# Moving ternary rounding, feature-attention normalisation and masked memory keys from VectorE to GpSimd

## The reference

```python
x = x + attention(layernorm(x))                  # 16 heads of 128, softmax over tokens
x = x + linear_attention(layernorm(x), ctx)      # relu features, divided by their sums
x = x + gated_ffn(layernorm(x))                  # weights quantised to nf4 and back
e = einsum('bci,bcj->bij', xn, xn)               # xn = layernorm(x)
x = x + einsum('bcj,bij->bci', xn, softmax(e))   # attention over features
x = x + gate * memory_attention(rmsnorm(layernorm(x)), ctx, mask)   # 16 heads of 16, 64 keys
x = x + ternary_ffn(layernorm(x))
```

```python
h = square(relu(h)); xmax = maximum(max(h, axis=-1), eps)
h = round(h / xmax * 255) / 255 * xmax
out = h @ w2.T
```

## Time and profile before

| | |
|---|---|
| median of 3 runs | 932.9 us (932.67 to 932.92) |
| the profiled execution, by its own count | 934.24 us |
| its span in the trace | 932.4 us |
| TensorE busy | 858.7 us, 92% |
| VectorE busy | 729.2 us, 78% |
| ScalarE busy | 520.5 us, 56% |
| GpSimd busy | 369.0 us, 40% |
| mean granted TensorE clock | 0.98 of full speed |

### The profile page before, as it was taken

How to read it: one execution, slowest core, us unless ns; L and a number is a source line. 1 busy time by engine, 2 the same in 40 slices (tenths; PEclk the granted TensorE clock), 3 DMA queues, 4 the chain that set the end, 5 groups by cost and what they waited for, 6 DMA issues and landing times. The chain is left out here.

```text
span 932.4 us, 18697 instructions
## 1 busy us (share of the span) xinstructions
PE 858.7 (92%) x6868; PEld 637.5 (68%) x6868; DVE 729.2 (78%) x1777; ACT 520.5 (56%) x1245; POOL 369.0 (40%) x356
## 2 busy tenths in 40 slices
PE   4798998999999999999999986999988889999786
PEld 3455766777777777777777765787856568777554
DVE  5738867878888788887887745898798879887895
ACT  1435576656665566656665643554364863535556
POOL 3104455545555555545554553044133031522410
PEclk9889999999999999999999997999999999999999
DMA  9022331011101111011100000000000010000001
GB/s 285 32 65 68 55 93 35 2 35 34 34 7 27 34 34 34 0 34 34 34 5 6 1 1 1 1 2 1 1 2 1 1 46 2 1 1 1 1 1 46
DMA packets 34722, 25.56 MB, mean 27 GB/s; under 512 B 9492, under 2 KB 31596, under 8 KB 34668
## 3 DMA queue, kind: packets, MB, share of 16 engines
q1 hardware_dynamic: 34380, 24.56, 10.1%
q10 hardware_dynamic: 288, 0.26, 0.1%
HBM read 22.65 MB, written 2.17 MB: 27 GB/s over the span
## 5 line engine op out<-in xcount | busy, mean ns | idle before, releaser
L476 POOL CAST exp_hi<-exp_scores 128x1024 f16<-128x1024 f32 x64 | 67.0, 1047 | 217.9 <-ACT exp_scores L580 217.9
L74 PE MATMUL banks<-value_out_hi,xn_t_hi 128*128 128x256 f16 x512 | 140.8, 275 | 2.3 <-DVE X L874 2.3
L478 POOL TENSOR_TENSOR exp_lo<-exp_scores,exp_hi 128x1024 f16<-128x1024 f32 x64 | 140.7, 2198 | 5.1
L580 ACT ACTIVATE exp_scores<-banks,exp_bias,unscale 128x256 f32<-128x256 f32 x256 | 141.0, 560 | 2.1
L75 PE MATMUL banks<-value_out_lo,xn_t_hi 128*128 128x256 f16 x512 | 140.6, 275 | 0.0
L76 PE MATMUL banks<-value_out_hi,xn_t_lo 128*128 128x256 f16 x512 | 140.6, 275 | 0.0
L1064 PE MATMUL banks<-qk 128*128 128x256 f32 x512 | 122.7, 383 | 9.9 <-ACT exp_scores L580 9.9
L1064 PEld LDWEIGHTS banks<-qk 128*128 128x128 f32 x512 | 97.2, 191 | 31.4 <-issue 10.5
L874 DVE SCALAR_TENSOR_TENSOR X<-banks,colsum,X 128x256 f32<-128x256 f32 x256 | 106.2, 477 | 11.0 <-DVE colsum L865 9.6
L562 ACT ACTIVATE qk<-banks 128x512 f32<-128x512 f32 x128 | 75.8, 601 | 59.1 <-PE banks L76 59.1
L853 DVE TENSOR_REDUCE neg_rowmax<-banks 128x4 f32<-128x1024 f32 x64 | 78.1, 1221 | 31.4 <-PE banks L1064 31.4
(11 more groups left out here) (238 smaller groups left out, 1965.9 us busy)
## 6 DMA issues: line engine op xcount, KB each, us to landing
head_weights<-in_wqkv_d SPq DMA_DIRECT2D x32, 128.0 KB, 3.7
weight_absmax_rows<-across_partitions SPq DMA_DIRECT2D x15, 256.0 KB, 4.1
X<-in_x_d SPq DMA_DIRECT2D x4, 512.0 KB, 7.5
head_weights<-in_wqkvt_d SPq DMA_DIRECT2D x16, 128.0 KB, 3.4
head_weights<-in_w_o_d SPq DMA_DIRECT2D x16, 128.0 KB, 3.5
out<-X SPq DMA_DIRECT2D x8, 256.0 KB, 2.1
res_then_ternary_then_kv<-in_c_fc_d SPq DMA_DIRECT2D x1, 1024.0 KB, 6.5
res_then_ternary_then_kv<-in_c_proj_d SPq DMA_DIRECT2D x1, 1024.0 KB, 8.2
```

What stands on the lines that cost most here:

```text
L74: nc.tensor.matmul(out, lhs[0], rhs[0], start=first, stop=False)
L476: nc.gpsimd.tensor_copy(probh[:, s1_.par], prob[:, s1_.par]).then_inc(exph_ready, 1)
L478: nc.gpsimd.tensor_tensor(probl[:, s1_.par], prob[:, s1_.par], probh[:, s1_.par], ALU.subtract).then_inc(expl_ready, 1)
L580: last = nc.scalar.activation(prob[:, s1_.par, t, :], sc_ps[t // ST][:, t % ST, :], ACT.Exp, bias=nbias[:, t:t + 1], scale=unscale[:, s1_. ...
```

## The change

Three steps are moved from VectorE to GpSimd. `fat_p` becomes one product of 128x512 with the two reciprocals spread over it. `mem_kbd` keeps its two products and gains explicit waits, one for the head mask and one for the sample's `fat_add`, which VectorE's order had implied. `n` is the same instruction on the other engine. The list of work names the new engine and new estimated lengths, so `turns_by_engine` gives new orders for all four engines.

```diff
--- before.py
+++ after.py
@@ -1235,10 +1235,10 @@
                 work += [f"ffn_{name}{m} {length} {after}"]
     work += [f"ffn_out PE 3.03 ffn_lo{FFT - 1}", "ffn_add DVE .67"]
     work += norm_work("fat", "ffn_add", ["xt ACT .49", "e PE 1.74 fat_xn"])
-    work += ["fat_max DVE .61", "fat_exp ACT .9", "fat_rsum DVE .08", "fat_p DVE .52", "fat_pt PE .45 fat_p fat_xt",
+    work += ["fat_max DVE .61", "fat_exp ACT .9", "fat_rsum DVE .08", "fat_p POOL 1.2", "fat_pt PE .45 fat_p fat_xt",
              "fat_pte ACT .49", "fat_out PE 1.83", "fat_add DVE .6"]
     work += norm_work("mem", "fat_add", ["xt ACT .74"])
-    work += ["mem_q PE 1.8", "mem_kbd DVE .67 fat_add", "mem_g PE 1.74 mem_xt", "mem_qt ACT .49 mem_q", "mem_ge ACT .49 mem_g"]
+    work += ["mem_q PE 1.8", "mem_kbd POOL 1.3 fat_add", "mem_g PE 1.74 mem_xt", "mem_qt ACT .49 mem_q", "mem_ge ACT .49 mem_g"]
     for t in range(ST):
         work += [f"mem{t}_{w}" for w in ("s PE 1.19" + (" mem_qt mem_kbd mem_ge" if t == 0 else ""),
                                          "max DVE 1.13", "sub DVE 1.14", "exp ACT .96", "sum DVE 1.13", "rd DVE .17",
@@ -1248,7 +1248,7 @@
     for t in range(ST):
         work += [f"ter{t}_{w}" for w in ("h PE 1.74" + (" ter0_nte ter0_add" if t else ""), "max DVE 1.13", "m0 DVE .12",
                                          f"relu ACT 1.0 ter{t}_max", f"c0 DVE .24 ter{t}_m0", "c1 DVE .08",
-                                         f"sq ACT 1.04 ter{t}_relu ter{t}_c1", "n DVE .6", "nt PE .45", "nte ACT .91",
+                                         f"sq ACT 1.04 ter{t}_relu ter{t}_c1", "n POOL 1.1", "nt PE .45", "nte ACT .91",
                                          "out PE .9", "add DVE .4")]
     turns = turns_by_engine(work)
 
@@ -1292,6 +1292,24 @@
                 pool.wait_ge(mem_rden[t], n[s])
                 nc.gpsimd.tensor_tensor(by_head(s), by_head(s), den[s][:, t, :].unsqueeze(2).broadcast_to([P, XH, M]),
                                         ALU.mult).then_inc(mem_pn[t], 1)
+            elif name == "fat_p":
+                pool.wait_ge(fat_rsum, n[s])
+                nc.gpsimd.tensor_tensor(att[s][:, :, :], att[s][:, :, :],
+                                        small[s][:, 2:4].unsqueeze(2).broadcast_to([P, KT, D]),
+                                        ALU.mult).then_inc(fat_p, 1)
+            elif name == "mem_kbd":
+
+                pool.wait_ge(mask4_ready, 1)
+                pool.wait_ge(fat["added"], n[s])
+                for k in range(KT):
+                    last = nc.gpsimd.tensor_tensor(
+                        kbd[s][:, k], g.k1t[:, k, M * s:M * (s + 1)].unsqueeze(1).broadcast_to([P, HK // 2, M]),
+                        g.mask4[:, :].unsqueeze(2).broadcast_to([P, HK // 2, M]), ALU.mult)
+                last.then_inc(mem_kbd, 1)
+            elif part == "n":
+                t = tile_of(layer)
+                pool.wait_ge(ter_sq[t], n[s])
+                nc.gpsimd.tensor_scalar(num[s], hid[s], ROUND, -ROUND, ALU.add, ALU.add).then_inc(ter_n[t], 1)
             elif name == "lin_bias":
 
                 pool.wait_ge(lin["xn"], n[s])
@@ -1499,22 +1517,9 @@
             elif name == "fat_rsum":
                 dve.wait_ge(fat_exp, n[s])
                 nc.vector.reciprocal(small[s][:, 2:4], small[s][:, 2:4]).then_inc(fat_rsum, 1)
-            elif name == "fat_p":
-                dve.wait_ge(fat_rsum, n[s])
-                for t in range(KT):
-                    last = nc.vector.tensor_scalar(att[s][:, t, :], att[s][:, t, :], small[s][:, 2 + t:3 + t], None,
-                                                   ALU.mult)
-                last.then_inc(fat_p, 1)
             elif name == "fat_add":
                 add_bank(s, fat_out, PB, "fat")
 
-            elif name == "mem_kbd":
-
-                for k in range(KT):
-                    last = nc.vector.tensor_tensor(
-                        kbd[s][:, k], g.k1t[:, k, M * s:M * (s + 1)].unsqueeze(1).broadcast_to([P, HK // 2, M]),
-                        g.mask4[:, :].unsqueeze(2).broadcast_to([P, HK // 2, M]), ALU.mult)
-                last.then_inc(mem_kbd, 1)
             elif name == "mem_go":
 
                 dve.wait_ge(mem_out, n[s])
@@ -1564,9 +1569,6 @@
                 dve.wait_ge(ter_step[s], s // STREAMS * 3 * ST + 3 * t + 2)
                 nc.vector.tensor_scalar(small[s][:, 7:8], small[s][:, 6:7], float(np.sqrt(255.0)), None,
                                         ALU.mult).then_inc(ter_scale[t], 1)
-            elif part == "n":
-                dve.wait_ge(ter_sq[t], n[s])
-                nc.vector.tensor_scalar(num[s], hid[s], ROUND, -ROUND, ALU.add, ALU.add).then_inc(ter_n[t], 1)
             elif part == "add":
                 dve.wait_ge(ter_step[s], s // STREAMS * 3 * ST + 3 * t + 3)
                 dve.wait_ge(ter_out[t], n[s])
```

## The result

The changed kernel takes **954.6 us** (median of 4 runs, 951.99 to 955.57) against 932.8 before (932.67 to 932.92): ratio **1.0234 [1.0216, 1.0252]**, 21.8 us slower. The prediction had 936.8 and a range to 940.5. The time moved the way that was forecast, but more than five times as far, and most of it for another reason than the one that the forecast priced.

A forecast was written before the change was run, and what follows sets the result against it. TensorE was taken to set the pace, except VectorE in memory attention and the four engines' hand-over in the ternary layer. Terms 1.4 + 0 + 2.5 = +3.9 us on 932.9 gave 936.8 us, range 932.0 to 940.5.

The forecast's parts named there:

- slow rival: Rounding costs 2.2 us or more on GpSimd and every collision is paid in full: 938.9 to 940.3 us; chance 0.12.
- collisions: VectorE's normalising pass waits for the GpSimd mask product of the same sample: 0 to 1.1 us for each sample.
- D's last transposes: Sample 7, end of last ternary layer: rounding's extra 0.4 us hides behind TensorE's order; at 2.2 us, 0.35 later.
- Place one: Between features and memory, each wave: mask product ahead of sample 3's scaling, pass collisions; +0.7 a wave, +1.4 in all.
- Place two: Between the waves: second wave's first samples fill TensorE, and a small delay is gained back; 0, bounds -0.5 and +1.4.
- Place three: Last wave's ternary layer: new orders delay additions, copies and second-half products; +2.5 us, bounds +1.0 and +3.5.
- No change: Rival: an earlier start of the ternary layer makes good the orders' losses there; 932.9 us, 931.0 to 934.8; chance 0.13.
- the sign that it asked for: No change's condition: VectorE's release before 680 us reaches the memory stretch, 2 to 3 us earlier.
- Faster: Rival: GpSimd starts roundings on time, reordering costs nothing, TensorE's 4.0 us of waits for roundings go: 928.9 us; chance 0.13.
- Slower still: The slow rival: rounding 2.2 us or more, collisions paid in full; 938.9 us, or 940.3 with place two; chance 0.12.
- the forecast's own walk: Step-by-step timing of the last wave's ternary layer, rounding taken as 1.1 us on GpSimd; it gave +2.5 us.

The follow-up runs named there:

- r_forms: The changed kernel with the rounding step in eight forms, by sample and half of the tokens; ran once, only instruction lengths read, no kernel time given.
- r_forms3: Third such kernel against the changed one: eight more forms of the instruction, f32 in, f16 out, 128x1024; ran once, only instruction lengths read.
- r_cast: The changed kernel with GpSimd's rounding replaced by a plain cast to f16 (1.04 us), all orders kept: 932.9 us, ratio 1.0009 against before.
- r_conv: The changed kernel with ScalarE's square written as 32-bit integers and GpSimd copying them to f16: 932.6 us, ratio 1.0009 against before.
- r_fma: The changed kernel with the rounding as one multiply-add on GpSimd, ScalarE's copy taking 1024 off: 933.3 us, ratio 1.0011 against before.
- r_two: The changed kernel with the rounding as two GpSimd copies, to 32-bit integers and back to f16 (2.08 us): 934.75 us, +2.8 against before.
- r_back: The changed kernel with the rounding back on VectorE, orders made anew; scalings and mask products stay on GpSimd: 933.0 us, ratio 1.0012 against before.
- r_none_moved: The kernel of r_none with scalings and mask products moved to GpSimd: 928.59 us, ratio 0.9949 against before.
- r_none_again: The same kernel as r_none, timed once more beside r_none_moved: 924.63 us, ratio 0.9915 against before.
- r_conv_last: As r_conv, with wave two's ternary layer in the order of before on TensorE, VectorE and ScalarE: 931.6 us, ratio 0.9999 against before.
- r_none: The kernel before without any rounding instruction: ScalarE writes 16-bit integers, TensorE transposes their bits, ScalarE's copy converts: 924.35 us, ratio 0.9910.

## Why the prediction was wrong

**The step that failed is one term: "Rounding, 128x1024 f32 to f16 with one input: the cast of that shape takes 1047 ns ... I take 1.1, nearest the cast (one input), and keep 1.05 to 2.2."** It was mis-sized by 2.5 us for each of 16 instructions. A cast and a two-operation arithmetic instruction share shape, types and the number of inputs, and the forecast took that to be enough. On GpSimd the operations decide (r_forms to r_forms3): the same shape costs 1.04 or 3.63. The bound of 2.2 was no bound either: it came from a row with a subtraction of two inputs, and an instruction with one input was taken to lie below it. No row of before had a tensor_scalar with arithmetic on that engine at this shape, so both ends were guesses. The slow rival said "2.2 us or more", but its time was worked out at 2.2, and "much more" had no price.
The Trainium skill (GPSIMD Engine Reference, 4.1 Engine selection) calls one-input work roughly line-rate, and its key points say that VectorE is about 2 times faster for elementwise work (1.37 us by that, an estimate). Neither agrees with 3.63 against 0.684 us, a factor of 5.3; the forms of 1.04 lie between.

**The direction was in the main luck.** The forecast's +3.9 was made of orders and collisions. With a rounding of 1.04 these gave +0.7 to +1.6 (r_cast, r_conv, r_fma), and over 20 of the 21.8 us came from a length that the forecast had hidden behind TensorE's order.

**What followed from a wrong size.** The text said that at 2.2 us D's last transposes start 0.35 later. That looked at one rounding, the last. r_two (2.08) lost 1.9 us in S against r_conv, and 1.5 of them lie before hA: four first-half roundings arrive close together, and the slow rival priced none of that. It also had the clock falling only as part of a bound of one microsecond, where the same matmuls took 9.1 us longer. In the change the last layer lost 11.0: hA starts 15.2 us after the last power, not 9.7 (+5.5), and from hA to the last addition it takes 26.3, not 20.8 (+5.5, in which hA at half clock is 1.7 longer and a wait for a rounding near the end is 3.07).

**Place one, +1.4 (0 to 2.5).** Right, in mechanism and nearly in size. The wait of 0.35 us before sample 3's transposes was seen (forecast 0 to 0.8), and so were the projection ahead of the output product and the collisions: where a pass met the mask products of its sample it took 1.0 to 1.3 us in place of 0.7, well under the upper bound. The waits are 1.6 (r_back against before) to 1.9 us (r_none_moved against r_none_again) for both waves. The 2.9 by which the second pair's P and R differ has 1.0 of longer matmuls in it, for which place one had no term.
The Trainium skill (SBUF — State Buffer, SBUF: two separate sides) calls the shared ports an exclusive lock for a whole instruction. The trace agrees, down to two columns: a step of 0.15 us took 1.73 and ended with the 1.90 of GpSimd. It does not bear out the full 1.1 that the prediction drew from it: with the first of the two mask products over, the pass went ahead, 0.3 to 0.6 us late. VectorE's row maxima, which read PSUM, kept their 1.22 us beside 14.4 us of GpSimd's roundings.

**Place two, 0 (-0.5 to +1.4).** Wrong: with a short rounding the new order gains 1.7 us there (Q, r_cast and r_conv_last). TensorE's idle time in Q and R together is 15.8 us in r_back and 14.3 to 14.4 in r_cast and r_conv. The prediction gave VectorE's 5.5 us of roundings no worth there, although in Q VectorE serves the first wave's ternary layer and the second wave's first layers at once. Whether the relief or the new order gains it, no run separates.

**Place three, +2.5 (1.0 to 3.5).** Right in sign, at the lower bound in size: +1.0 (r_conv against before), and r_conv_last takes it away again. r_cast's S alone (+2.6) had seemed to confirm 2.5; 1.6 of it was a dip. The three places together, read as TensorE's idle time, come to +1.0 (32.4 before, 33.4 to 33.6 in r_cast, r_conv and r_fma): +1.1 in P, -1.1 in Q and R, +0.9 in S.

**Rivals.** No change was what the moves gave with a short rounding (+0.7 to +1.6 in r_cast, r_conv and r_fma), and the sign that it asked for was there: counted from the first power, the last layer starts 328.1 us on in before, 327.0 in r_conv and 325.9 in r_cast. But that came through Q, where 1.7 us were gained, and through a dip in R that before has and these two have not, and not through the memory stretch. Faster saw rightly that waits for roundings could go: without the instruction 5.0 us of idle time went (7.4 us of time), where the rival had 4.0; but moving it to GpSimd gives none of that. Slower still had the right cause and a third of its size: the time was 14 us beyond its 940.3.

With 3.63 in the place of 1.1 the forecast's own walk would have shown the direction of the miss: the first rounding starts 4.4 us after the wave's last power and B's ends 7.3 later, and behind it TensorE makes B's transposes (0.6), outA (1.04) and, after VectorE's addition (0.5), hA: not before 13.8, where it started at 9.7. That is an estimate of +4.1 a wave without any clock, from the rows above, and 8 of the 21.8 us; the later queues and the clock are not in it.

## What to carry to other kernels

Price an instruction on another engine by a row with the same operations, not only the same shape, types and inputs; where none exists, keep the upper end open and say what the kernel does at three times the price. When a step on the path to TensorE gets longer, its waits grow evenly with it (here 4 to 5 us for each microsecond, with 16 such steps), and from some length on TensorE's idling is paid again in its clock: so look at both, idle and busy time, before explaining a kink. Before moving a step, ask whether a conversion that a neighbour makes anyway can do it: here ScalarE's output type takes its place.

## What was not expected of the hardware

- On GpSimd (128x1024, f32 in) multiply-then-add, its reverse and two multiplications take 1.04 us, one operation 2.77, other pairs 3.63.
- ScalarE can write its squares as 16-bit integers in the time of the f32 output (1.15 us for 128x1024 in r_none and before), and TensorE's transposes carry their bits through to PSUM (r_none). Whether that conversion rounds to the nearest number or cuts off, no run shows.
- The two profiles of one kernel, r_none and r_none_again, differ by a dip in P (1.41 us: 150.75 and 149.34) and one in Q (1.60: 22.94 and 21.34). TensorE behind the same wait of 2.07 us, in r_none:

```profile
723.39 0.66 PE L1599 MATMUL banks<-ident,xn_stream 128*128 128x128 f32 x4 [2.07 <-DVE xn_stream L1436]
723.99 5.31 PE L1742 MATMUL banks<-ternary,xt_stream 128*128 128x512 f16 x16
```

and in r_none_again:

```profile
720.24 0.65 PE L1599 MATMUL banks<-ident,xn_stream 128*128 128x128 f32 x4 [2.07 <-DVE xn_stream L1436]
720.85 3.63 PE L1742 MATMUL banks<-ternary,xt_stream 128*128 128x512 f16 x16
```

The same sixteen matmuls take 5.31 or 3.63 us. Such a dip stands in one to three of the four stretches in most profiles here, so one pair of profiles cannot price a term below some 1.6 us by its length: the cut has to be compared dip by dip, or by medians of ten runs. TensorE's idle time is steadier: over the four stretches it is 27.3 us in r_none and 27.4 in r_none_again, while the busy time is 325.8 and 322.5.
